# Transposing second attention's first rows one product earlier, and giving each row tile of the last expert block its own PSUM bank

## The chip, the cores and the metric

The kernel runs on one core of a Trainium2 chip. Time is device time in microseconds (us) for one execution; lower is better. TensorE (PE) multiplies, VectorE (DVE) and ScalarE (ACT) work elementwise, GpSimd (POOL) does small arithmetic and issues the indirect DMAs, SyncE (SP) issues the other DMAs. Each engine works through its own instructions in the order in which they are written; semaphores are all that ties the engines together.

## What is computed

Two layers of a gated network over `x` of 4 batches x 1024 tokens x 256. The lines that matter here:

```
x = x + tanh(g_xattn[0]) * L0_xattn(layernorm(x), ctx)      # first attention
x = x + tanh(g_ffn[0])   * L0_ffn(layernorm(x))             # 8 experts, top 2 of each token
x = x + tanh(g_xattn[1]) * L1_xattn(layernorm(x), ctx)      # second attention: 16 heads, 77 keys
x = x + tanh(g_ffn[1])   * L1_ffn(layernorm(x))             # 8 experts, each takes its 256 best tokens

# second attention
sim  = einsum('bhid,bhjd->bhij', x @ Wq, ctx @ Wk) * SCALE
out  = softmax(sim) @ (ctx @ Wv);   return out @ Wo + bo
# second expert layer
out.at[bidx, idx].add(gating * ((silu(x_in @ Wg) * (x_in @ Wu)) @ Wd))
```

## The kernel before, in words

The program has six stages in each engine's stream, one after another: first attention, first experts, a stage named `prep_*` that prepares weights for second attention, second attention (`attn1_*`), the rest of a choice of tokens (`topk_*`), second experts (`ffn1_*`). Nothing but semaphores separates the stages.

All products are made of half-precision pieces. A value v becomes a high piece (ACT copies it to f16) and a low piece (DVE subtracts the high one from v), and `mm3` (L121 to L126) multiplies high by high, high by low and low by high: three matmuls on lines L124, L125, L126. So almost every tile goes PE -> ACT -> DVE before the next product can read it.

**The end of `prep_*`.** For each batch b and half m, PE forms `M1` (folded query and key weights, in four banks `psM`) and then "turns" v of the output weights, `N1` (folded value and output weights), each in one of four banks `psN`. Turns 0 and 1 belong to m = 0, turns 2, 3 and 4 to m = 1. Turn 4, the last one, is the product over the 13 left-over keys of each head and takes 24 matmuls of 256 columns; turns 2 and 3 take 6 each. ACT makes the high piece of each turn (L1336, semaphore `u_nh`), DVE the low piece (`outputs_low`, L1382, semaphore `u_nl`). When b = 3 is complete, `u_nl` stands at 20.

**The beginning of `attn1_*`.** Rows go through in 32 tiles t of 128 tokens. For a tile: DVE takes statistics of the row tile (`stats`, `moments`), POOL makes 1/std (`rstd_of`, L1651 and L1653), DVE normalises (`normalise`, L1859, tile `xn`), PE transposes (L1760, tile `psXar`, whose first half is called `psXa`), ACT and DVE make the pieces `xh` (`high_in`, L1695) and `xl` (`low_in`, L1865), PE forms the scores in two halves (`scores0`, `scores1`, tile `psS`), DVE takes each head's largest score (`largest`, L1880) and ACT the exponentials (`exps`, L1720); then POOL divides (`normalise_probs`, tile `pn`), PE transposes the probabilities (L1798) and multiplies by `N1` (tile `psOL`).

Each engine's order within a step is a table written by hand (`PE_ORDER`, `ACT_ORDER`, `DVE_ORDER`, `POOL_ORDER`) of names with a lag: an entry with lag 2 handles tile t - 2 in step t. In PE's table `scores1` has lag 0 and `scores0` lag 1, so tile 0's half 1 is the first product of the stage, then come the transposes of tile 1, then tile 0's half 0. In DVE's table tile 0's `largest1` stands in step 2, behind `normalise_in` of tile 1 (step 1) and `stats_in` and `moments_in` of tile 2.

Tile 0's statistics and normalisation stand ahead of the tables, woven into the last turns:

```
stats(0)(0, 0)
moments(0)(0, 0)
outputs_low(dve, B - 1, N_TURNS[KD - 1][0])
normalise(0)(0, 0)
for v in N_TURNS[KD - 1][1:]:
    outputs_low(dve, B - 1, v)
```

POOL has, after the 1/std of tile 0 and ahead of the 1/std of tile 1, a wait for all output weights and six small set-up instructions:

```
rstd_of(0)(0, 0)
pool.wait_ge(u_nl, 5 * B)
```

**The end of `ffn1_*`.** The 16 expert blocks have 512 gathered rows each, that is four row tiles n of 128. `down` multiplies the hidden values by the down weights, 24 matmuls of 256 columns for each row tile, into `psYb`, which has four tiles of 128x256 in two PSUM banks: tiles 0 and 1 in one, 2 and 3 in the other. PE and ACT don't touch one bank at the same time, so PE reports (`d_y`) after tiles 1 and 3, and ACT (`results`, L2220) then scales two tiles each into `yo` and reports each (`d_yo`). POOL (`add`, L2118) waits for each row tile's `d_yo` and issues one indirect DMA that adds its rows to `out_x`. Ahead of a block's four adds POOL waits until all adds of the block before have landed (`d_out`). `psXb` is the two-bank tile in which gathered rows are transposed; its last use is for block 15's rows, ahead of that block's up product.

Of the kernel before, what the change touches and what calls it, by code (L numbers as in the profile page):

```python
# [28 lines left out]
ACT = mybir.ActivationFunctionType  # L29
AX = mybir.AxisListType  # L30

P = 128
# [17 lines left out]
SV = 64.0  # L50
# [95 lines left out]
def program(nc, a, out, tab, n0_rows, x1_rows, n_rows):  # L146
    ctx = ExitStack()
    with ctx:
# [1099 lines left out]
        def prep_tensor(pe):  # L1248
# [20 lines left out]
            for b in range(B):  # L1269
                keys = slice(b * LK, (b + 1) * LK)  # L1270
                for m in range(KD):
                    for bank in range(4):
# [7 lines left out]
                        last.then_inc(u_m, 1)  # L1280
                    for v in N_TURNS[m]:
                        if b == 0 and v < 4:
                            pe.wait_ge(u_pl, HP + max(2 * v + 2, v + 5))
                            pe.wait_ge(u_z, 4)
                        wait(pe, u_nl, 5 * b + v - 3)
                        o = psN[(5 * b + v) % 4]
                        for i in range(2):
                            if v < 4:
                                pair = 2 * v + i
                                last = mm3(pe, o[:, i, :], V1[0][:, pair, b, :], V1[1][:, pair, b, :],  # L1290
                                           woh[:, pair * D:(pair + 1) * D], wol[:, pair * D:(pair + 1) * D], True, True)
                                continue
                            first = i * (HP // 2)
                            for pair in range(first, first + HP // 2):
                                last = mm3(pe, o[:, i, :], V2[0][:, pair, b, :], V2[1][:, pair, b, :],
                                           woh[:, pair * D:(pair + 1) * D], wol[:, pair * D:(pair + 1) * D],
                                           pair == first, pair == first + HP // 2 - 1)
                        last.then_inc(u_n, 1)

        def prep_scalar(act):  # L1300
# [20 lines left out]
            for b in range(B):  # L1321
                for m in range(KD):
# [11 lines left out]
                    for v in N_TURNS[m]:  # L1334
                        act.wait_ge(u_n, 5 * b + (v + 1))
                        act.activation(N1[:, b, 2 * v:2 * v + 2, 0:D], psN[(5 * b + v) % 4][:, :, :], ACT.Copy,  # L1336
                                       scale=SV / (SK * SW)).then_inc(u_nh, 1)

# [351 lines left out]
        def attn1_scalar(act):  # L1690
# [52 lines left out]
            steps = dict(weights_high=weights_high, shares_exp=shares_exp, shares_copy=shares_copy,  # L1743
                         high_in=high_in, copy_out=copy_out, exps0=exps(0), exps1=exps(1),
                         probs_high0=probs_high(0), probs_high1=probs_high(1),
                         probs_high2=probs_high(2))
            in_order(act, steps, ACT_ORDER, T, straight=True)

        def attn1_tensor(pe):
# [75 lines left out]
            def digit_odd(t, par):  # L1825
                if odd_of(t) is not None:
# [3 lines left out]
            N1f = N1[:].rearrange("p b c d -> p (b c d)")  # L1830
            steps = dict(tail_a=tail("a"), tail_b=tail("b"), digit_odd=digit_odd, transposes_in=transposes(0), transposes_out=transposes(1), scores0=scores(0), scores1=scores(1),
                         turn0=turn(0), turn1=turn(1), turn2=turn(2), logits=logits,
# [4 lines left out]
        def attn1_vector(dve):  # L1837
# [14 lines left out]
            def normalise(n):  # L1852
                def run(t, par):
# [7 lines left out]
                return run  # L1861

            def low_in(t, par):
# [50 lines left out]
            normalise(0)(0, 0)  # L1914
            for v in N_TURNS[KD - 1][1:]:
                outputs_low(dve, B - 1, v)
            def shares_max(t, par):
# [57 lines left out]
            def weights_low(t, par):  # L1975
                f = t - 4
                if not 0 <= f < FT1:
# [12 lines left out]
                         normalise_in=after_first(normalise(0)), normalise_out=normalise(1), stats_in=after_first(stats(0)), stats_out=stats(1),  # L1990
                         moments_in=after_first(moments(0)), moments_out=moments(1), low_in=low_in,
                         residual=residual, reciprocals=reciprocals)
# [48 lines left out]
                 (7, "n1"): FILL, (7, "n2"): TURN}  # L2041
        ONE_HOT_STEP = 7

        def later(step, name):
# [79 lines left out]
        def ffn1_tensor(pe):  # L2124
# [28 lines left out]
            def down(j, ph):  # L2153
# [3 lines left out]
                for n in range(NT):  # L2157
                    if n % 2 == 0:
                        wait(pe, d_yo, NT * (j - 1) + n + 2 if not isinstance(j, int) or j > 0 else 0)
                    rows = slice(n * P, (n + 1) * P)  # L2160
                    for f in range(FT1):
                        at = f * D
                        last = mm3(pe, psYb[:, n, :], hh1[:, par, f, rows], hl1[:, par, f, rows], W1dh[:, par, at:at + D],
                                   W1dl[:, par, at:at + D], f == 0, f == FT1 - 1)
                    if n % 2 == 1:
                        last.then_inc(d_y, 1)
# [8 lines left out]
        def ffn1_scalar(act):  # L2175
# [36 lines left out]
            def results(j, ph):  # L2212
                par = ph % 2
                if not isinstance(j, int) or j >= 2:
                    act.wait_ge(d_out[par], 16 * NT * (j // 2))
                act.wait_ge(d_gate, j + 1)
                for n in range(NT):
                    if n % 2 == 0:
                        act.wait_ge(d_y, 2 * j + (n // 2 + 1))
                    act.activation(yo1[:, par, n, :], psYb[:, n, :], ACT.Copy, scale=gsc[:, ph, n:n + 1]).then_inc(d_yo, 1)  # L2220

# [177 lines left out]
```

## Time and profile before

| | |
|---|---|
| time, three runs | 1417.0, 1421.34, 1421.36 us, median 1421.34 |
| the profiled execution's own time | 1407.95 us |
| its span in the trace | 1406.2 us, so 1.75 us lie outside the span |
| PE busy | 1297.4 us (92%) |
| DVE, ACT, POOL busy | 911.0, 761.5, 627.0 us |
| mean granted TensorE clock | 0.945 of full speed |

The profile is of one execution. In a timeline a row gives the start and the duration in us, the engine, the line of the kernel, what is written and read, how many instructions the row merges, and in brackets how long the engine had been idle and which engine's instruction ended that wait. A row of windows gives a stretch of the span, its length, the busy time (and number of instructions) of PE, PEld (weight loads), DVE, ACT and POOL in this order, the TensorE clock that was granted (1.00 is 2.4 GHz, 0.50 is 1.2 GHz), the share of DMA busy and GB/s.

### The profile page before, as it was taken

The numbers are of one execution on the slowest core, as the hardware profiler recorded it, in microseconds if no ns is written. First come the engines' busy times: TensorE is split into PE (matmuls) and PEld (weight loads), VectorE is DVE, ScalarE is ACT, GpSimd is POOL, SyncE is SP. The second block draws the span as 40 slices with busy tenths as digits, with TensorE's granted clock in tenths as the row PEclk, the third lists the DMA queues.
The fourth block names the chain that finished last, engine by engine and source line by source line (L and its number), as shares of the span: only waits on it lengthen the run. The fifth ranks groups of instructions, "written<-read, shape, count | busy, mean of one in ns | idle before, by whom it ended". The sixth has DMA issues, their size and how long they took to land.

```text
span 1406.2 us, 29217 instructions
## 1 busy us (share of the span) xinstructions
PE 1297.4 (92%) x9858; PEld 975.7 (69%) x9859; DVE 911.0 (65%) x2128; ACT 761.5 (54%) x2315; POOL 627.0 (45%) x664
## 2 busy tenths in 40 slices
PE   7966699999999999899999985899999999999997
PEld 3755588879999968788888773356656666566555
DVE  2887664565555577778776885777776555566651
ACT  3775332432332365988887752655645555555551
POOL 2177678666666540454444433133333333333113
PEclk8675599999999999999999996999999999999999
DMA  4657444654334351100210103244444444444322
GB/s 146 213 163 184 96 50 56 122 109 67 63 60 64 63 142 40 39 32 32 91 39 24 34 31 93 106 120 121 121 121 124 150 158 148 126 130 129 108 45 31
DMA packets 81546, 133.17 MB, mean 95 GB/s; under 512 B 24662, under 2 KB 71260, under 8 KB 76316
## 3 DMA queue, kind: packets, MB, share of 16 engines
q1 hardware_dynamic: 51132, 93.92, 20.1%
q0 software_dynamic: 29312, 37.57, 16.5%
q8 instruction: 61, 1.00, 0.3%
q14 instruction: 49, 0.40, 0.1%
q10 hardware_dynamic: 992, 0.27, 0.1%
HBM read 95.08 MB, written 36.65 MB: 94 GB/s over the span
## 4 chain that ended last, share of the span: by engine, by line
PE 70%; DVE 10%; DMA 6%; issue 5%; POOL 5%; ACT 2%; SPq 0%; POOLq 0%; ACTq 0%; DVEq 0%
PE psG L124 5%; PE psG L126 5%; PE psG L125 5%; PE psU L124 5%; PE psU L126 5%; PE psU L125 5%; PE psYb L124 4%; PE psYb L125 4%; PE psYb L126 4%; DMA stage<-in_w 3%; PE psP L1798 2%; PE psS L124 2%; PE psS L125 2%; PE psS L126 2%; PE psOL L126 2%
## 5 line engine op out<-in xcount | busy, mean ns | idle before, releaser
L2118 POOL DMA_INDIRECT out_x<-yo,gidx x64 | 100.2, 1566 | 324.0 <-ACT yo L2220 310.8
L2268 DVE SCALAR_TENSOR_TENSOR hid<-psU,sil 128x512 f32<-128x512 f32 x128 | 88.4, 691 | 167.2 <-ACT sil L2209 166.7
L980 POOL DMA_INDIRECT x_rows<-yo,tabs x78 | 124.7, 1599 | 91.7 <-ACT yo L1052 68.0
L1720 ACT ACTIVATE pr<-psS,mx 128x77 f32<-128x77 f32 x512 | 158.8, 359 | 5.2 <-DVE mx L1889 5.2
L2209 ACT ACTIVATE sil<-psG 128x512 f32<-128x512 f32 x128 | 76.4, 597 | 118.1 <-PE psU L126 118.1
L126 PE MATMUL psYb<-W1dh,hl 128*128 128x256 f16 x512 | 139.6, 273 | 0.0
L125 PE MATMUL psYb<-W1dl,hh 128*128 128x256 f16 x512 | 139.6, 273 | 0.0
L124 PE MATMUL psYb<-W1dh,hh 128*128 128x256 f16 x512 | 139.6, 273 | 0.0
L1079 DVE SCALAR_TENSOR_TENSOR hid<-psU,sil 128x512 f32<-128x512 f32 x78 | 53.8, 690 | 127.3 <-ACT sil L1043 127.2
L1720 ACT ACTIVATION_READ_ACCUMULATOR pr<-psS,mx 128x1 f32 x512 | 123.6, 242 | 0.0
L1043 ACT ACTIVATE sil<-psG 128x512 f32<-128x512 f32 x78 | 46.5, 596 | 134.2 <-PE psU L126 132.2
L970 POOL DMA_INDIRECT bx<-n_rows,tabs x78 | 84.6, 1084 | 26.0 <-issue 22.6
L1651 POOL TENSOR_SCALAR rs<-mv 128x1 f32<-128x1 f32 x64 | 14.2, 222 | 180.8 <-DVE mv L1849 180.7
L2103 POOL DMA_INDIRECT gx<-n_rows,gidx x64 | 68.4, 1068 | 47.4 <-DVE gxl L2261 23.6
L124 PE MATMUL psG<-bxh,Wh 128*128 128x256 f16 x312 | 85.7, 275 | 3.9 <-DVE bxl L1070 3.9
L2220 ACT ACTIVATE yo<-psYb,gsc 128x256 f32<-128x256 f32 x64 | 26.8, 470 | 115.1 <-PE psYb L126 115.1
L124 PE MATMUL psOL<-N,pt 128*128 128x256 f16 x320 | 87.3, 273 | 0.7 <-DVE pt L1872 0.7
L125 PE MATMUL psOL<-N,pt 128*128 128x256 f16 x320 | 87.2, 273 | 0.0
L126 PE MATMUL psOL<-N,pt 128*128 128x256 f16 x320 | 87.2, 273 | 0.0
L2281 DVE TENSOR_TENSOR hl<-hid,hh 128x512 f16<-128x512 f32 x128 | 87.2, 681 | 0.0
L125 PE MATMUL psG<-bxl,Wh 128*128 128x256 f16 x312 | 85.7, 275 | 0.0
L126 PE MATMUL psG<-bxh,Wl 128*128 128x256 f16 x312 | 85.7, 275 | 0.0
(407 smaller groups left out, 4331.1 us busy)
## 6 DMA issues: line engine op xcount, KB each, us to landing
w1u<-in_w SPq DMA_DIRECT2D x16, 2048.0 KB, 7.4
w1d<-in_w SPq DMA_DIRECT2D x16, 1024.0 KB, 9.7
stage<-in_w SPq DMA_DIRECT2D x8, 1536.0 KB, 8.9
X<-in_x SPq DMA_DIRECT2D x8, 512.0 KB, 8.6
n_rows<-xc SPq DMA_DIRECT2D x8, 512.0 KB, 9.0
x_rows<-X SPq DMA_DIRECT2D x8, 512.0 KB, 10.2
X<-x_rows SPq DMA_DIRECT2D x8, 512.0 KB, 8.0
out_x<-X SPq DMA_DIRECT2D x32, 128.0 KB, 1.7
```

Of the source, the lines that this page charges most:

```text
L124: pe.matmul(o, lh, rh, start=first, stop=False)
L125: pe.matmul(o, lh, rl, start=False, stop=False)
L126: return pe.matmul(o, ll, rh, start=False, stop=stop)
L970: pool.indirect_dma_start(bx[:, par, n, :], None, n0_rows[:, :], bass.IndirectOffsetOnAxis(tabs[:, j, n, 0:1], 0)).then_inc(b_in[par], 16)
L980: pool.indirect_dma_start(x1_rows[:, :], bass.IndirectOffsetOnAxis(tabs[:, j, n, 0:1], 0), yo[:, par, n, :], None, compute_op=ALU.add).the ...
L1079: dve.scalar_tensor_tensor(hid[:, half, :, :], psU[half][:, :, :], SH / (SX * SW), sil[:, half, :, :], ALU.mult, ALU.mult).then_inc(b_hid[ ...
L1720: ins = act.activation(pr1[:, par, h * LK:(h + 1) * LK], psS1[:, q, i * LK:(i + 1) * LK], ACT.Exp, bias=mx1[:, h:h + 1], scale=1.0 / (SX * ...
L2103: pool.indirect_dma_start(gx[:, j % 2, n, :], None, n_rows[0:2 * S * (j // E + 1), :], bass.IndirectOffsetOnAxis(gidx[:, half, col:col + 1 ...
L2118: pool.indirect_dma_start(out_rows[:, :], bass.IndirectOffsetOnAxis(gidx[:, half, col:col + 1], 0), yo1[:, j % 2, n, :], None, compute_op= ...
L2209: act.activation(sil1[:, f % 2, :], psG1[f % 2][:], ACT.Silu, scale=1.0 / (SX * SW)).then_inc(d_sil, 1)
L2268: dve.scalar_tensor_tensor(hid1[:, f % 2, :], psU1[f % 2][:], SH / (SX * SW), sil1[:, f % 2, :], ALU.mult, ALU.mult).then_inc(d_hid, 1)
L2281: dve.tensor_tensor(hl1[:, par, f, :], hid1[:, f % 2, :], hh1[:, par, f, :], ALU.subtract).then_inc(d_hl, 1)
```

## The change

Part one, at the seam between `prep_*` and `attn1_*`: PE's two transposes of tile 0 are issued ahead of turn 4 of batch 3, not behind it, and wait for `c_xn[0]` (tile 0 normalised) and for `u_nl` at 17 (bank free). ACT's `high_in` of tile 0 stands ahead of the high piece of turn 4, and DVE's `low_in` of tile 0 between the low pieces of turns 3 and 4. The tables skip tile 0 for these three. Part two, in the last expert block only: row tiles 0 to 3 go into four banks (`psYb` twice, `psXb` twice), PE reports after each of them, and ACT waits for each.

```
--- before.py
+++ after.py
@@ prep_tensor
                     for v in N_TURNS[m]:
+                        if b == B - 1 and v == 4:
+                            pe.wait_ge(c_xn[0], 1)
+                            pe.wait_ge(u_nl, 5 * b + 2)
+                            for k in range(KD):
+                                last = pe.transpose(psXa[:, k, :], xn1[0][:, 0, k * P:(k + 1) * P], ident[:])
+                            last.then_inc(c_xt[0], 1)
                         if b == 0 and v < 4:
@@ prep_scalar
                     for v in N_TURNS[m]:
-                        act.wait_ge(u_n, 5 * b + (v + 1))
-                        act.activation(N1[:, b, 2 * v:2 * v + 2, 0:D], psN[(5 * b + v) % 4][:, :, :], ACT.Copy,
-                                       scale=SV / (SK * SW)).then_inc(u_nh, 1)
+                        if b < B - 1 or v < 4:
+                            outputs_high(act, b, v)
@@ attn1_scalar
+            high_in(0, 0)
+            outputs_high(act, B - 1, 4)
             in_order(act, steps, ACT_ORDER, T, straight=True)
@@ attn1_vector
-            for v in N_TURNS[KD - 1][1:]:
-                outputs_low(dve, B - 1, v)
+            outputs_low(dve, B - 1, 3)
+            low_first()
+            outputs_low(dve, B - 1, 4)
@@ ffn1
+        def result(j, n):
+
+            if j == NB1 - 1:
+                return (psYb[:, 0, :], psYb[:, 2, :], psXb[:, 0, 0:D], psXb[:, 1, 0:D])[n]
+            return psYb[:, n, :]
@@ ffn1_tensor, down
                 for n in range(NT):
-                    if n % 2 == 0:
+                    if j == NB1 - 1:
+                        pe.wait_ge(d_yo, NT * (j - 1) + 2 * min(n, 1) + 2)
+                    elif n % 2 == 0:
                         wait(pe, d_yo, NT * (j - 1) + n + 2 if not isinstance(j, int) or j > 0 else 0)
...
-                    if n % 2 == 1:
+                    if n % 2 == 1 or j == NB1 - 1:
                         last.then_inc(d_y, 1)
@@ ffn1_scalar, results
                 for n in range(NT):
-                    if n % 2 == 0:
+                    if j == NB1 - 1:
+                        act.wait_ge(d_y, 2 * j + n + 1)
+                    elif n % 2 == 0:
                         act.wait_ge(d_y, 2 * j + (n // 2 + 1))
```

In PE's stream, at the end of `prep_*` (psN2 and psN3 are the banks of turns 3 and 4, psXar that of the transposes, xn10 tile 0 normalised), the change puts the two transposes (x2) between the products of turns 3 and 4:

```order
 L125 MATMUL psN2<-wo1l,V1h 128x256
 L126 MATMUL psN2<-wo1h,V1l 128x256
+L1286 MATMUL psXar<-ident,xn10 128x128 x2
 L124 MATMUL psN3<-wo1h,V2h 128x256
 L125 MATMUL psN3<-wo1l,V2h 128x256
```

They stood on line L1760 behind the 24 matmuls of turn 4, directly ahead of the first scores.

DVE's stream from tile 0's statistics to tile 0's first `largest`, before the change (psN1, psN2 and psN3 are the banks of turns 2, 3 and 4; `st10`, `mv10`, `rs10`, `xn10` belong to the normalisation in front of the scores):

```order
L1843 BN_STATS st10<-X 128x6
L1849 BN_AGGR mv10<-st10 128x2
L1382 SCALAR_TENSOR_TENSOR N1<-psN1,N1 128x2x256
L1859 TENSOR_SCALAR xn10<-X,mv10,rs10 128x256
L1382 SCALAR_TENSOR_TENSOR N1<-psN2,N1 128x2x256
L1382 SCALAR_TENSOR_TENSOR N1<-psN3,N1 128x2x256
L1843 BN_STATS st10<-X 128x6
L1849 BN_AGGR mv10<-st10 128x2
L1865 SCALAR_TENSOR_TENSOR xl1<-psXar,xh1 128x256
L1859 TENSOR_SCALAR xn10<-X,mv10,rs10 128x256
L1843 BN_STATS st10<-X 128x6
L1849 BN_AGGR mv10<-st10 128x2
```

And the same stretch of the changed kernel, up to that `largest`:

```order
L1393 SCALAR_TENSOR_TENSOR N1<-psN2,N1 128x2x256
L1881 SCALAR_TENSOR_TENSOR xl1<-psXar,xh1 128x256
L1393 SCALAR_TENSOR_TENSOR N1<-psN3,N1 128x2x256
L1856 BN_STATS st10<-X 128x6
L1862 BN_AGGR mv10<-st10 128x2
L1872 TENSOR_SCALAR xn10<-X,mv10,rs10 128x256
L1856 BN_STATS st10<-X 128x6
L1862 BN_AGGR mv10<-st10 128x2
L1896 TENSOR_REDUCE psS1<-psS1 128x2x4
L1905 TENSOR_SCALAR mx1<-psS1 128x8
```

The low piece of tile 0 (`xl1`) has moved ahead of turn 4's low piece; all else keeps its order. POOL's stream is the same in both.

## Rows read from the trace of the kernel before

**Rows 1.** The page: the span, and each engine's busy time.

```profile
span 1406.2 us, 29217 instructions
PE 1297.4 (92%) x9858; PEld 975.7 (69%) x9859; DVE 911.0 (65%) x2128; ACT 761.5 (54%) x2315; POOL 627.0 (45%) x664
```

**Rows 2.** Windows, all of second attention.

```profile
555.00:850.00 295.00, 273.93 (x2322) 230.75 (x2319) 231.38 (x614) 228.06 (x1198) 132.48 (x233) 0.99 0.13 43
```

**Rows 3.** Timeline of PE at the seam.

```profile
552.46 0.27 PE L124 MATMUL psN<-wo1h,V2h 128*128 128x256 f16 x1
...
554.97 0.27 PE L126 MATMUL psN<-wo1h,V2l 128*128 128x256 f16 x1
556.04 0.41 PE L1760 MATMUL psXar<-ident,xn 128*128 128x128 f32 x2 [0.79 <-DVE xn L1859]
558.00 0.44 PE L124 MATMUL psS<-M1h,xh 128*128 128x308 f16 x1 [1.55 <-DVE xl L1865]
...
561.06 0.45 PE L1760 MATMUL psXar<-ident,xn 128*128 128x128 f32 x2
561.35 0.29 PE L124 MATMUL psS<-M1h,xh 128*128 128x308 f16 x1
...
565.05 0.29 PE L124 MATMUL psS<-M1h,xh 128*128 128x308 f16 x1 [1.97 <-ACT pr L1720]
```

**Rows 4.** Timeline of POOL at the seam.

```profile
557.15 0.20 POOL L1678 MEMSET ones<- 128x128 bf16 x1 [1.71 <-DVE N L1382]
...
558.92 0.58 POOL L1653 TENSOR_TENSOR rs<-rs,mhalf 128x1 f32<-128x1 f32 x1
```

**Rows 5.** Timeline of DVE at the seam.

```profile
555.48 0.42 DVE L1859 TENSOR_SCALAR xn<-X,mv,rs 128x256 f32<-128x256 f32 x1 [0.45 <-POOL rs L1653]
555.80 1.28 DVE L1382 SCALAR_TENSOR_TENSOR N<-psN,N 128x512 f16<-128x512 f32 x2
...
559.53 0.41 DVE L1859 TENSOR_SCALAR xn<-X,mv,rs 128x256 f32<-128x256 f32 x1 [1.59 <-POOL rs L1653]
...
560.32 0.18 DVE L1849 BATCH_NORM_AGGREGATE mv<-st 128x2 f32<-128x6 f32 x1
561.30 0.81 DVE L1880 TENSOR_REDUCE psS<-psS 128x8 f32<-128x616 f32 x1 [0.80 <-PE psS L126]
```

**Rows 6.** Timeline of ACT at the seam: turn 4's high piece.

```profile
555.28 0.60 ACT L1336 ACTIVATE N<-psN 128x512 f16<-128x512 f32 x1 [1.70 <-PE psN L126]
```

**Rows 7.** The chain that ended last, one piece (start, us, what).

```profile
562.35 2.57 ACT pr L1720 x16
```

**Rows 8.** Windows of 1 us at the seam, columns as in rows 2.

```profile
557.00:558.00 1.00, 0.00 (x0) 0.00 (x0) 0.91 (x4) 0.00 (x0) 0.64 (x4) 0.89 0.00 0
558.00:559.00 1.00, 1.00 (x4) 0.59 (x5) 0.00 (x0) 0.00 (x0) 0.69 (x5) 0.50 0.01 4
...
561.00:562.00 1.00, 1.00 (x9) 0.80 (x8) 0.70 (x1) 0.38 (x1) 0.46 (x1) 0.91 0.92 393
```

**Rows 9.** Windows around PE's longest wait, at second attention's end, columns as in rows 2.

```profile
845.00:850.00 5.00, 0.00 (x0) 0.00 (x0) 4.86 (x5) 0.00 (x0) 0.00 (x0) 0.79 0.00 0
850.00:855.00 5.00, 3.98 (x26) 3.85 (x26) 2.17 (x6) 0.38 (x1) 0.79 (x2) 0.50 0.15 52
```

**Rows 10.** Timeline of ACT at the very end: the last two row tiles.

```profile
1395.82 0.84 ACT L2220 ACTIVATE yo<-psYb,gsc 128x256 f32<-128x256 f32 x2 [4.32 <-PE psYb L126]
```

**Rows 11.** Timeline of POOL at the very end: the adds.

```profile
1387.93 1.54 POOL L2118 DMA_INDIRECT out_x<-yo,gidx  x1 [0.30 <-issue]
1392.93 1.54 POOL L2118 DMA_INDIRECT out_x<-yo,gidx  x1 [3.46 <-DMA out_x<-yo,gidx]
...
1396.62 1.54 POOL L2118 DMA_INDIRECT out_x<-yo,gidx  x1 [0.30 <-ACT yo L2220]
1398.46 1.54 POOL L2118 DMA_INDIRECT out_x<-yo,gidx  x1 [0.30 <-issue]
```

**Rows 12.** The DMAs that write out_x: from issue to landing.

```profile
DMA to landing us min/median/max: 1.7/3.8/8.3
```

More of the change, by code:

```diff
@@ L1334, in prep_scalar, with outputs_high @@
                     for v in N_TURNS[m]:
-                        act.wait_ge(u_n, 5 * b + (v + 1))
-                        act.activation(N1[:, b, 2 * v:2 * v + 2, 0:D], psN[(5 * b + v) % 4][:, :, :], ACT.Copy,
-                                       scale=SV / (SK * SW)).then_inc(u_nh, 1)
+                        if b < B - 1 or v < 4:
+                            outputs_high(act, b, v)
+        def outputs_high(act, b, v):
+            act.wait_ge(u_n, 5 * b + (v + 1))
+            act.activation(N1[:, b, 2 * v:2 * v + 2, 0:D], psN[(5 * b + v) % 4][:, :, :], ACT.Copy,
+                           scale=SV / (SK * SW)).then_inc(u_nh, 1)
         def prep_vector(dve):
@@ L1743, in attn1_scalar @@
             steps = dict(weights_high=weights_high, shares_exp=shares_exp, shares_copy=shares_copy,
-                         high_in=high_in, copy_out=copy_out, exps0=exps(0), exps1=exps(1),
+                         high_in=after_first(high_in), copy_out=copy_out, exps0=exps(0), exps1=exps(1),
                          probs_high0=probs_high(0), probs_high1=probs_high(1),
                          probs_high2=probs_high(2))
+            high_in(0, 0)
+            outputs_high(act, B - 1, 4)
             in_order(act, steps, ACT_ORDER, T, straight=True)
@@ L1830, in attn1_tensor @@
             N1f = N1[:].rearrange("p b c d -> p (b c d)")
-            steps = dict(tail_a=tail("a"), tail_b=tail("b"), digit_odd=digit_odd, transposes_in=transposes(0), transposes_out=transposes(1), scores0=scores(0), scores1=scores(1),
+            steps = dict(tail_a=tail("a"), tail_b=tail("b"), digit_odd=digit_odd, transposes_in=after_first(transposes(0)), transposes_out=transposes(1), scores0=scores(0), scores1=scores(1),
                          turn0=turn(0), turn1=turn(1), turn2=turn(2), logits=logits,
@@ L1861, in normalise, with low_first @@
                 return run
+            def low_first():
+                low_in(0, 0)
             def low_in(t, par):
@@ L1990, in attn1_vector @@
                          normalise_in=after_first(normalise(0)), normalise_out=normalise(1), stats_in=after_first(stats(0)), stats_out=stats(1),
-                         moments_in=after_first(moments(0)), moments_out=moments(1), low_in=low_in,
+                         moments_in=after_first(moments(0)), moments_out=moments(1), low_in=after_first(low_in),
                          residual=residual, reciprocals=reciprocals)
@@ L2162, in down @@
                         at = f * D
-                        last = mm3(pe, psYb[:, n, :], hh1[:, par, f, rows], hl1[:, par, f, rows], W1dh[:, par, at:at + D],
+                        last = mm3(pe, result(j, n), hh1[:, par, f, rows], hl1[:, par, f, rows], W1dh[:, par, at:at + D],
                                    W1dl[:, par, at:at + D], f == 0, f == FT1 - 1)
-                    if n % 2 == 1:
+                    if n % 2 == 1 or j == NB1 - 1:
                         last.then_inc(d_y, 1)
@@ L2217, in results @@
                 for n in range(NT):
-                    if n % 2 == 0:
+                    if j == NB1 - 1:
+                        act.wait_ge(d_y, 2 * j + n + 1)
+                    elif n % 2 == 0:
                         act.wait_ge(d_y, 2 * j + (n // 2 + 1))
-                    act.activation(yo1[:, par, n, :], psYb[:, n, :], ACT.Copy, scale=gsc[:, ph, n:n + 1]).then_inc(d_yo, 1)
+                    act.activation(yo1[:, par, n, :], result(j, n), ACT.Copy, scale=gsc[:, ph, n:n + 1]).then_inc(d_yo, 1)
             def hidden_high(f):
```

## The prediction

> **What bounds the kernel now.** I read the page first. TensorE is busy 1297.4 of 1406.2 us [rows 1], so whatever holds PE up at a place where nothing else is queued for it lengthens the kernel. A second look, at the windows, says how far that holds in second attention: 273.9 of 295 us busy [rows 2]. So a delay at the mouth of that stage is carried to its end, since PE has little slack in which to win it back. Both parts of the change lie where the average doesn't reach: at a seam between two stages and in the last microseconds. So the views to use are the timelines of each engine there, together with the releaser in brackets.
>
> At the seam, PE's timeline [rows 3] shows turn 4 of the output weights from 552.46 to 555.24 (last start 554.97 plus 0.27), a wait of 0.79 for `xn` of tile 0, the transposes at 556.04, a wait of 1.55 for `xl`, and then the first twelve score matmuls from 558.00 to 561.06. Those twelve take 0.255 us each; the next twelve start at 561.35 and end at 563.08 (565.05 less the wait of 1.97), 0.131 each. The windows of the same stretch explain it: the granted clock falls to half at about 557.8 (0.89 of the window 557 to 558), is 0.50 at 558 to 559 and comes back at about 561.2 [rows 8]. This is what the change seems made for: two waits and a half-clock stretch around the first scores.
>
> But what set the time of everything behind? The first `largest` of DVE starts at 561.30 and has waited 0.80 for PE [rows 5]; from there the chain runs through sixteen instructions of exponentials at 562.35 [rows 7] and on to POOL's division. So the stage's clock is the start of that `largest`, and it has two inputs. One is PE's scores. The other is DVE's own queue: ahead of it stand `xn` of tile 1 (559.53, having waited 1.59 for POOL's 1/std) and the statistics of tile 2, done at 560.32 + 0.18 = 560.50 [rows 5]. This second input is only 0.80 us behind the first.
>
> Where does the 1/std of tile 1 come from? POOL first waits for all output weights (`u_nl` at 20), released by the low piece of turn 4, which ends at 555.80 + 1.28 = 557.08; its set-up starts at 557.15 and tile 1's 1/std is done at 558.92 + 0.58 = 559.50 [rows 4, 5]. So there is a path turn 4 -> high piece -> low piece -> six set-up instructions and 1/std on POOL -> `xn` of tile 1 -> statistics of tile 2 -> `largest` of tile 0. The change delays the head of this path.
>
> **Part one, step by step.** *The transposes.* They are put ahead of turn 4 but need `xn` of tile 0, which ends at 555.48 + 0.42 = 555.90 [rows 5]. Nothing ahead of that on DVE or POOL is touched. So they start at 556.04 as before. PE, which had begun turn 4 at 552.46, now stands idle from there to 556.04: 3.6 us of work that used to lie in the shadow of this wait (2.8 of it turn 4) is pushed behind it. Matmuls keep their written order, so turn 4 can't slip past.
>
> *Turn 4.* It starts behind the transposes, 0.29 later as at 561.06 to 561.35 [rows 3]: 556.33. Its length is bounded from both sides. At full clock it takes its 2.78 and ends at 559.1. At half clock throughout, its starts spread by the ratio of the score matmuls, 0.255 / 0.131 = 1.95: 2.51 x 1.95 + 0.3 = 5.2, end at 561.5. Which? A wait of 1.97 left the clock full (565.05); waits of 0.79 and 1.55 with 0.41 of work between brought it to half, and so did the longest wait, from before 845 to after 850 [rows 3, 8, 9]. The new wait, 3.3 us unbroken (552.7 to 556.04), is nearer to the two that cost the clock. If it falls where it fell before, at 557.8, 13 of the 24 run at 0.109 and the rest at 0.213, and turn 4 ends at 560.2; I take a little more, 560.3.
>
> *Its pieces.* ACT starts the high piece 0.04 after PE ends and takes 0.60 [rows 6]; DVE's low piece follows in about 0.03 and 0.68 (two took 1.28 [rows 5]). That is 1.35, so `u_nl` stands at 20 at 560.45, 561.6 or 562.9 for the three ends, against 557.08.
>
> *POOL and what is queued behind.* The step to POOL's first set-up instruction is 0.07; from there to DVE being free for `largest` it was 560.50 - 557.15 = 3.35 [rows 4, 5], and none of that changes. So `largest` starts at 563.9, 565.0 or 566.3, against 561.30: **+2.6, +3.7 or +5.0 us**. The 0.80 that `largest` used to wait for PE is already in these differences.
>
> *PE's side.* The first scores now follow turn 4 without a wait (their `xl` is made at about 557.3, under turn 4), and even at half clock end 3.2 us after it, at 564.7 against a `largest` at 566.3. So PE is no longer what ends that wait. This is the gain that the change is to bring: with a full clock the scores end at 560.7, not 561.2. It buys nothing, because DVE isn't there yet. PE then waits for `xn` of tile 1 before the second transposes, at about 563.3 at the earliest, and only then makes tile 0's other scores. These take 1.7 us at full clock, ending at 565.4, at half clock at 566.9. The first exponentials run until 1.05 + 2.57 after the first `largest` starts [rows 5, 7], until 567.5; the second half needs 1.05 from its scores to its exponentials, so it is ready at 566.5 or 568.0. This adds 0 to 0.5; I take 0.
>
> *Covered pieces.* `high_in` ahead of turn 4's high piece on ACT and `low_in` ahead of its low piece on DVE (0.4 us each) cost nothing: both run while PE is in turn 4. If turn 4 were done by then, they would cost 0.8. SP also waits for `u_nl`: the bias row and the first load of second expert weights leave some 4 us later; the first is needed by tile 0's last outputs and the second some steps on, and neither ends a wait now.
>
> **Part two.** The last block's tiles would be copied one at a time, so tiles 0 and 2 earlier by one tile's product (24 x 0.109 = 2.6 us), tile 1 no earlier, and tile 3 from 1395.82 + 0.84 to + 0.48 [rows 10]. But POOL's four last adds start at 1392.93, released by the landing of block 14's last add (issued 1387.93), and follow at 1.84 apiece to 1398.46 [rows 11]. Tile 2's add at 1396.62 came when POOL was free (1394.77 + 1.54 + 0.30), and its tile was ready at 1395.82 + 0.42 + 0.3 = 1396.5. So the early tiles would wait for POOL; the gain is 0 to 0.1. POOL's pace is bounded by a landing: here 4.73 (1387.93 to 0.27 before 1392.93), elsewhere 1.7 to 8.3, median 3.8 [rows 12]. With 3.8 the four would start at 1392.0, tile 2's add no longer would wait for PE, and the change would gain 0.9. If the landing is short enough, tile 3 itself decides: add at 1395.82 + 0.48 + 0.3 = 1396.6, not 1398.46, a gain of at most 1.8.
>
> The Trainium skill, DMA: Bandwidth & Descriptors, section Anatomy of one DMA, gives a DMA issued from GpSimd about 2.0 us fixed and bytes over 436 GB/s; for 128 rows of 1 KB that is 2.3 us, and by it the full 1.8 us would be gained here. This case's trace disagrees: 4.73 us for this very add.
>
> **The sum.** Part one +3.7, part two 0: the profiled execution would go from a span of 1406.2 to 1409.9, and with the 1.75 outside it from 1407.95 to 1411.65. That execution is 13 us faster than the median of the timed runs, 1421.34; the seam is a chain of compute durations, so I carry the difference over as it is: 1425.0 us.
>
> **Rivals.**
> *A, half clock almost throughout (slower, +4.3 to +5.5).* The new wait costs the clock before turn 4 begins, and perhaps again in the wait before the second transposes. For it: the length of the wait. Against: the half-clock stretch before lasted 3.4 us, so turn 4 may get its end at full clock. It decides once turn 4 ends after 560.8. 1425.6 to 1426.8.
> *B, the cover pays (not slower).* Scores end at 560.7, the wait for `xl` is gone, and the stage starts 0.5 to 0.7 earlier: 1420.7. The point from which it decides is POOL: its wait for `u_nl` at 20 would have to end by 557.4 (560.8 less 3.35 and 0.07), and for any gain at all by 557.9. Turn 4 is still under way then. I leave it a chance only for what the trace may hide, such as a wait that isn't where I read it.
> *C, the tail gives back 0.9 to 1.8.* A landing nearer the median than the 4.73 of this add: +3.7 less the middle of the two, 1423.6; with a full clock and the whole 1.8, +0.8, 1422.1. The figure of the Trainium skill (above) would put the time at this end.
> *D, neither part shows.* Should DVE or POOL win the delay back inside second attention: 1421.3. Against it: 93% busy PE.
>
> **How the numbers follow.** About 0.3%, 4.3 us, is what a measurement of this kernel can tell from no change (its three runs span 4.4). Forecast (+2.6 to +4.3) 0.50; A 0.28; C 0.10; B 0.05; D 0.07. The range 1420.0 to 1428.5 holds A and C whole and the scatter of a median above A; below it lies what is left of B and D with scatter. Slower by over 0.3%: most of A and a part of the forecast's upper half, 0.37. Within: 0.57. Faster by over 0.3%: only scatter on B, C or D, 0.06.
>
> **What the profile after would show.** Right: PE idle about 3.3 us ahead of the transposes, released by `xn`; turn 4 behind them; no wait of the first scores for `xl`; POOL's first set-up at 560.5 to 563; DVE's first `largest` behind the statistics of tile 2, not behind PE, at 564 to 566; PE waiting for `xn` of tile 1; POOL's four last adds still 1.84 apart, their first released by a landing. Wrong: `xn` of tile 0 well before 555.9 after the stage's start, which would make the move free; a first `largest` within 1 us of where it was; or a tail whose adds wait for tiles.

## The result, and the profile after

| | median | runs |
|---|---|---|
| before | 1418.33 us | 1416.21 to 1421.48, 20 runs |
| changed kernel | 1423.88 us | 1420.04 to 1426.46, 20 runs |

The ratio is 1.0038, with a 95% interval of 1.003 to 1.0045: **the change costs 5.5 us (4.3 to 6.4)**. The forecast was +3.7 on a median of 1421.34, which is 1425.0; the measured 1423.88 lies in the range of 1420.0 to 1428.5. One timed execution of all kernels below stood apart, 2899.41 us in e9, and is in no ratio.

The profiled execution of the changed kernel has a span of 1420.3 us, 14 more than the one before. Most of this says nothing about the change: tile 0's normalisation, which comes ahead of everything that was moved, starts at 565.32 in the one and at 555.48 in the other [rows 5], and over all the profiles below it lies anywhere from 553.5 to 571.8. So every seam here is measured from that instruction; its start is called x0. The rest of the comparison is made with differences from x0.

The timeline of PE at the seam of the changed kernel (start, duration, line, tile, in brackets the idle time and its releaser):

```profile
562.19 0.27 PE L126 MATMUL psN<-wo1h,V1l 128*128 128x256 f16 x1
565.79 0.56 PE L1286 MATMUL psXar<-ident,xn 128*128 128x128 f32 x2 [3.32 <-DVE xn L1872]
566.14 0.42 PE L124 MATMUL psN<-wo1h,V2h 128*128 128x256 f16 x1
...
569.34 0.30 PE L124 MATMUL psN<-wo1h,V2h 128*128 128x256 f16 x1
...
570.24 0.27 PE L126 MATMUL psN<-wo1h,V2l 128*128 128x256 f16 x1
570.35 0.29 PE L124 MATMUL psS<-M1h,xh 128*128 128x308 f16 x1
...
574.78 0.44 PE L1773 MATMUL psXar<-ident,xn 128*128 128x128 f32 x2 [2.70 <-DVE xn L1872]
...
578.91 0.29 PE L124 MATMUL psS<-M1h,xh 128*128 128x308 f16 x1 [2.12 <-ACT pr L1731]
```

It answers to rows 3. The two short waits (0.79 and 1.55) are gone, and the scores at 570.35 start without one. In their place stand one wait of 3.32 ahead of the transposes, a turn 4 whose matmuls start 0.21 apart for the first 15 and 0.11 apart after that, and a wait of 2.70 for tile 1's normalisation. The windows of 1 us show the clock (the column ahead of the last two) at half under turn 4, and once more at 580:

```profile
565.00:566.00 1.00, 0.21 (x2) 0.22 (x3) 0.68 (x2) 0.00 (x0) 0.28 (x1) 0.98 0.00 0
566.00:567.00 1.00, 1.00 (x7) 0.69 (x6) 0.53 (x2) 0.38 (x1) 0.00 (x0) 0.50 0.06 16
...
569.00:570.00 1.00, 1.00 (x9) 0.82 (x8) 0.00 (x0) 0.00 (x0) 0.00 (x0) 0.81 0.00 0
570.00:571.00 1.00, 1.00 (x10) 0.79 (x9) 0.00 (x0) 0.45 (x1) 0.00 (x0) 1.00 0.00 0
...
580.00:581.00 1.00, 1.00 (x5) 0.61 (x4) 0.00 (x0) 1.00 (x8) 0.00 (x0) 0.50 0.00 0
```

Now what the rest waited for. The timeline of POOL, then that of DVE:

```profile
571.93 0.20 POOL L1689 MEMSET ones<- 128x128 bf16 x1 [6.65 <-DVE N L1393]
...
573.70 0.58 POOL L1664 TENSOR_TENSOR rs<-rs,mhalf 128x1 f32<-128x1 f32 x1
```

```profile
565.32 0.41 DVE L1872 TENSOR_SCALAR xn<-X,mv,rs 128x256 f32<-128x256 f32 x1 [0.45 <-POOL rs L1664]
...
571.18 0.69 DVE L1393 SCALAR_TENSOR_TENSOR N<-psN,N 128x512 f16<-128x512 f32 x1 [3.95 <-ACT N L1347]
...
574.31 0.41 DVE L1872 TENSOR_SCALAR xn<-X,mv,rs 128x256 f32<-128x256 f32 x1 [1.90 <-POOL rs L1664]
...
575.10 0.18 DVE L1862 BATCH_NORM_AGGREGATE mv<-st 128x2 f32<-128x6 f32 x1
575.20 0.78 DVE L1896 TENSOR_REDUCE psS<-psS 128x8 f32<-128x616 f32 x1
```

Read it as one path: low piece of turn 4 at 571.18, POOL's first set-up at 571.93 (it had waited 6.65 for it), tile 1's 1/std done at 574.28, `xn` of tile 1 at 574.31, the first `largest` at 575.20. That `largest` has no bracket: nothing but its own queue held it, while PE's scores had long been there (the last of them starts at 571.79). In before it waited 0.80 for PE [rows 5]. From x0 it is 9.88 us, against 5.82.

The second-attention stage then carries the delay to its end. The line of the residuals (one for each of the 32 row tiles, first and last start), before:

```profile
L1905 DVE SCALAR_TENSOR_TENSOR X<-psOL,thx,X x32: 447/478/486, 579.0 to 850.2; 128x256 f32<-128x256 f32 x32
```

and in the changed kernel:

```profile
L1921 DVE SCALAR_TENSOR_TENSOR X<-psOL,thx,X x32: 450/478/486, 593.7 to 864.9; 128x256 f32<-128x256 f32 x32
```

Less x0 the last is at 294.7 before and 299.6 after: +4.9 us, of which 4.06 are the first `largest` and 0.8 come behind it. The rest of the program passes this on: from there to the end of the span it is 556.0 us before (1406.2 less 850.2) and 555.4 after (1420.3 less 864.9).

At the very end, POOL's adds of the changed kernel:

```profile
1402.70 1.54 POOL L2141 DMA_INDIRECT out_x<-yo,gidx  x1 [0.30 <-issue]
1407.21 1.54 POOL L2141 DMA_INDIRECT out_x<-yo,gidx  x1 [2.96 <-DMA out_x<-yo,gidx]
...
1412.74 1.54 POOL L2141 DMA_INDIRECT out_x<-yo,gidx  x1 [0.30 <-issue]
```

ACT's last four copies, now one at a time, start at 1402.81, 1405.35, 1407.97 and 1410.59. The adds don't follow them: the first is released by the landing of block 14's last add, as in [rows 11], and the last starts 2.15 after the last tile's copy starts, against 2.27 before (1398.46 less 1396.19; the row of 1395.82 in [rows 10] merges two copies).

### The profile page after: what moved, and what is told of

It is laid out like the page before. It is cut to its first block, busy times and chain, and to the rows that moved or that the text cites. A ratio compares the mean times of both kernels' runs of the same rounds, so it can differ in the third digit from the quotient of the medians.

```text
span 1420.3 us, 29218 instructions
## 1 busy us (share of the span) xinstructions
PE 1300.5 (92%) x9858; PEld 976.1 (69%) x9859; DVE 911.7 (64%) x2128; ACT 760.7 (54%) x2315; POOL 625.2 (44%) x664
## 4 chain that ended last, share of the span: by engine, by line
PE 72%; DVE 11%; DMA 5%; issue 4%; POOL 4%; ACT 3%; another core or an unknown queue 1%; SPq 0%; DVEq 0%; ACTq 0%; POOLq 0%
PE psG L124 6%; PE psG L126 5%; PE psG L125 5%; PE psU L125 5%; PE psU L124 5%; PE psU L126 5%; PE psYb L124 4%; PE psYb L126 4%; PE psYb L125 4%; PE psP L1811 2%; PE psS L124 2%; PE psS L126 2%; PE psS L125 2%; DMA stage<-in_w 2%; PE psOL L126 2%
## 5 line engine op out<-in xcount | busy, mean ns | idle before, releaser
L126 PE MATMUL psYb<-W1dh,hl 128*128 128x256 f16 x496 | 135.2, 273 | 0.0
L125 PE MATMUL psYb<-W1dl,hh 128*128 128x256 f16 x496 | 135.2, 273 | 0.0
L124 PE MATMUL psYb<-W1dh,hh 128*128 128x256 f16 x496 | 135.2, 273 | 0.0
L124 PE MATMUL psY<-Wh,hh 128*128 x312 | 85.1, 273 | 1.0 <-issue 0.9
L126 PE MATMUL psU<-bxh,Wl 128*128 128x256 f16 x312 | 85.6, 274 | 0.1
L125 PE MATMUL psU<-bxl,Wh 128*128 128x256 f16 x312 | 85.6, 274 | 0.1
```

Source lines behind the costliest of these rows:

```text
L124: pe.matmul(o, lh, rh, start=first, stop=False)
L125: pe.matmul(o, lh, rl, start=False, stop=False)
L126: return pe.matmul(o, ll, rh, start=False, stop=stop)
```

## The experiments

All but one were timed against before on the same chip, in rounds. The table gathers what each trace shows, from x0 where not said otherwise; "clock" is what the granted clock was under the first long product behind the new or the old wait. "Last residual" is the end of the seam's reach, "last add" the start of the program's last add after the start of the last tile's copy. A ratio rests on 12 executions of the kernel, in e2 on 5, in e3 on 11, in e10 on 7. The groups of runs had different chips, so ratios compare across groups and times don't.

| run | ratio to before (95%) | clock | first `largest` | last residual | last add |
|---|---|---|---|---|---|
| before | | half | 5.82 | 294.7 | 2.27 |
| before, second trace (e11) | | half | 5.81 | 294.7 | 2.63 |
| changed kernel | 1.0038 (1.003 to 1.0045) | half, 3.4 us | 9.88 | 299.6 | 2.15 |
| e1 part two alone | 0.9995 (0.9985 to 1.0004) | half | 5.82 | 294.7 | 2.10 |
| e2 part one alone | 1.0038 (1.0025 to 1.0051) | half throughout | 10.91 | 299.8 | 2.22 |
| e3 + tile 1 early | 1.0014 (1.0002 to 1.0027) | half throughout | 8.10 | 297.9 | |
| e4 + wait filled | 1.0037 (1.0024 to 1.0051) | full | 8.22 | 297.9 | |
| e5 both of these | 1.0000 (0.9983 to 1.0017) | full | 5.35 | 295.0 | |
| e10 as e3, POOL as changed | 1.0043 (1.002 to 1.0066) | full | 8.22 | 297.9 | |
| e6 before, DVE and POOL order | 0.9987 (0.9972 to 1.0002) | full | 3.71 | 292.6 | |
| e7 before, banks for two blocks | 0.9980 (0.9964 to 0.9997) | full | 4.95 | 293.8 | 0.75 |
| e8 e6, e7 and filled waits | 0.9986 (0.997 to 1.0003) | full | 3.71 | 292.6 | 1.03 |
| e9 e6 and e7 | 0.9987 (0.9969 to 1.0004) | half | 5.08 | 294.0 | 0.75 |
| e12 e8 again | 0.9975 (0.9959 to 0.999) | full | 3.71 | 293.6 | 1.04 |

**e1, part two alone.** Before with the second half of the diff.

> Part two alone: before, with only the last block's four row tiles in four banks. Theory S (the loss is all at the seam): no measurable change, 0 to 0.9 us faster; the four last adds start by a landing and follow 1.84 apart. Rival T (some of the 5.5 us come from the tail, for instance copies that meet the matmuls of another bank): slower by 1 to 5 us, with a gap between the last adds.

Measured: no change can be seen (1405.49 against 1406.03 us). The adds start 1.84 apart behind a landing, the last at 1398.20, though ACT had the tiles one by one. There is nothing of the loss at this end, nor a gain that can be told from zero (the interval leaves 2.1 us faster to 0.6 slower): Theory S holds, Rival T is out.

**e2, part one alone.** The changed kernel with the old end.

> Part one alone: the changed kernel with the old tail. Theory S: as slow as the whole change, 4.5 to 5.5 us above before; first largest 9.9 us after the start of tile 0's normalisation, against 5.8 before. Rival T: 0 to 3 us above before.

Measured: 1412.02 against 1406.03 us, the whole of the loss. Here the clock was low from ahead of turn 4 to its end and the first `largest` came at 10.91, a microsecond later than expected. With a landing 0.7 shorter than in before (4.01, not 4.73), two tiles to a bank do show: the third add waits for its tile.

```profile
1396.39 1.54 POOL L2141 DMA_INDIRECT out_x<-yo,gidx  x1 [2.73 <-DMA out_x<-yo,gidx]
1398.23 1.54 POOL L2141 DMA_INDIRECT out_x<-yo,gidx  x1 [0.30 <-issue]
1400.75 1.54 POOL L2141 DMA_INDIRECT out_x<-yo,gidx  x1 [0.97 <-ACT yo L2247]
```

That 0.67 (0.97 less 0.30) is an estimate of what part two can be worth in such an execution; the times don't show it.

**e3, tile 1 early.** Does the delay travel through POOL and tile 1? The changed kernel, with (tables skip tile 1 too):

```
@@ POOL
             rstd_of(0)(0, 0)
+            rstd_of(0)(1, 1)
             pool.wait_ge(u_nl, 5 * B)
@@ DVE
             outputs_low(dve, B - 1, 3)
+            stats(0)(1, 1)
+            moments(0)(1, 1)
             low_first()
+            normalise(0)(1, 1)
             outputs_low(dve, B - 1, 4)
```

> The changed kernel, but tile 1's statistics, 1/std and normalisation stand ahead of turn 4's low piece on DVE and ahead of the wait for all output weights on POOL. Theory S (the delayed turn 4 reaches DVE's first largest through POOL and tile 1): first largest then follows PE's scores, 6.9 us after the start of tile 0's normalisation (9.9 in the changed kernel, 5.8 in before); time 1 to 2 us above before, 3 to 4 below the changed kernel. Rival C (the half clock of turn 4 and of the scores is what costs, POOL's path is only seen beside it): largest stays at 9 to 10 us and the time within 1 us of the changed kernel.

Measured: 1408.09 against 1406.03 us, +0.14% where the changed kernel has +0.38%, so some 60% of the loss is gone by the ratios. (The trace is of the slowest of the 11 executions, and in it the last residual is 1.7 earlier than in the changed kernel's, a third of the 4.9.) Tile 1 is normalised at 2.58 and no longer in the way. The number for `largest` was missed, 8.10 instead of 6.9, because the clock was at half throughout and turn 4 ended a microsecond later than in the changed kernel. DVE's rows also show something that Theory S had left out:

```profile
563.40 0.69 DVE L1401 SCALAR_TENSOR_TENSOR N<-psN,N 128x512 f16<-128x512 f32 x1 [3.95 <-ACT N L1355]
564.01 0.42 DVE L1865 BATCH_NORM_STATS2 st<-X 128x6 f32<-128x256 f32 x1
564.46 0.18 DVE L1871 BATCH_NORM_AGGREGATE mv<-st 128x2 f32<-128x6 f32 x1
564.56 0.78 DVE L1905 TENSOR_REDUCE psS<-psS 128x8 f32<-128x616 f32 x1
```

`largest` has no bracket. With tile 1 out of the way it stands directly behind turn 4's low piece and the statistics of tile 2, about 0.2 behind PE's scores (564.08 + 0.29 = 564.37). So the low piece is an obstacle by itself, a small one.

**e4, the wait filled.** The changed kernel, with work for PE while it waits for `xn`:

```
@@ PE, ahead of the transposes
                         if b == B - 1 and v == 4:
+                            pe.wait_ge(u_nl, 5 * b + v - 3)
+                            for f in range(28):
+                                pe.matmul(psN[(5 * b + v) % 4][:, f % 2, :], V2[0][:, f % HP, b, :],
+                                          woh[:, (f % HP) * D:(f % HP + 1) * D], start=True, stop=True)
                             pe.wait_ge(c_xn[0], 1)
```

> The changed kernel with 28 matmuls of 256 columns more, whose results are overwritten, in PE's wait ahead of the transposes, so that the wait is filled with work. Theory S: turn 4 runs at full clock (2.8 us, not 4.7), all else of the path stays, so the first largest comes 8.4 us after the start of tile 0's normalisation (9.9 without them) and the time is 1.5 to 2.5 us below the changed kernel, still 2.6 to 3.5 above before. Rival C: with the clock kept, all of the loss is gone, 0 to 1 us above before. A third case: the clock is lost all the same, time as the changed kernel.

Measured: in the trace it does what Theory S says. The wait shrinks to 0.26, turn 4 runs at full clock, `largest` comes at 8.22 (expected 8.4), and the last residual is at 297.9, 3.3 later than before:

```profile
553.99 0.44 PE L1290 MATMUL psXar<-ident,xn 128*128 128x128 f32 x2 [0.26 <-DVE xn L1876]
554.27 0.27 PE L124 MATMUL psN<-wo1h,V2h 128*128 128x256 f16 x1
554.38 0.27 PE L125 MATMUL psN<-wo1l,V2h 128*128 128x256 f16 x1
```

So the clock alone doesn't explain the loss (Rival C is out). But the timed runs, 1412.10 against 1406.03, don't show the 1.5 to 2.5 us below the changed kernel. The two intervals, 1.0024 to 1.0051 here and 1.003 to 1.0045 there, leave room for no more than 3 us; the trace's difference in last residual, 1.7 us (0.12%), is within them, the same time for both is nearer their middle. e2, with the same seam and timed beside e4 on one chip, has 1412.02. The gain from filling is seen in the trace and not in the times. Why the times don't show it stays open: the clock of the executions without a trace isn't known stretch by stretch.

**e5, both.** The changed kernel with e3's and e4's edits.

> The changed kernel with both mendings: tile 1's statistics and normalisation ahead of turn 4's low piece, and the 28 overwritten matmuls in PE's wait. Theory S: turn 4 starts 0.6 after the start of tile 0's normalisation and ends at 3.6, the scores at 5.0, and the first largest starts at 5.1 to 5.3 (before 5.8, changed kernel 9.9 to 10.9); the stage's last residual 0.7 us earlier to 0.3 later than before, or up to 1 us later if PE's clock falls once more behind it; time within 1 us of before. Rival C: POOL's path doesn't matter beside the clock; then this is as the kernel with the filled wait alone, 3.3 us later than before in the trace.

Measured: 1420.87 against 1420.45 us, ratio 1.0000 (0.9983 to 1.0017): with both mended the loss is gone. `largest` comes at 5.35 behind the low piece and two statistics, not behind the scores; the last residual at 295.0, 0.4 later than before although `largest` was 0.5 earlier, since PE's clock fell once more further on (0.50 at 11 to 12 after x0). Rival C would have had 3.3. What the filling adds to e3's edit isn't clear of zero in the times: the intervals of e3 and e5 overlap.

**e10, POOL's order put back.** Is it POOL's wait, or DVE's statistics behind the low piece? e3 with this:

```
@@ POOL
             rstd_of(0)(0, 0)
-            rstd_of(0)(1, 1)
             pool.wait_ge(u_nl, 5 * B)
...
             ch.end()
+            rstd_of(0)(1, 1)
@@ DVE
-            normalise(0)(1, 1)
             outputs_low(dve, B - 1, 4)
+            normalise(0)(1, 1)
```

> The run e3 with one thing put back: POOL makes tile 1's 1/std behind its wait for all output weights, as in before and in the changed kernel (DVE's normalisation of tile 1 therefore behind turn 4's low piece; its statistics stay early). Theory S: the link is POOL's wait, so all of what e3 won is lost: first largest 3.3 us after POOL's first set-up instruction, at 9.9 to 10.9 after the start of tile 0's normalisation, and the time 4 to 6 us above before. Rival D (the link is DVE's statistics of tile 1 behind the low piece, not POOL): largest at 7 to 8.1 as in e3, time 1 to 3 above before.

Measured: 1415.20 against 1409.57 us, ratio 1.0043 (e3 1.0014; the intervals just overlap, from 1.002 to 1.0027), all of what e3 won is lost. In its trace the statistics of tile 1 are done at 556.33 + 0.18, five microseconds ahead of their use, and still:

```profile
561.67 0.58 POOL L1672 TENSOR_TENSOR rs<-rs,mhalf 128x1 f32<-128x1 f32 x1
```

```profile
562.28 0.41 DVE L1881 TENSOR_SCALAR xn<-X,mv,rs 128x256 f32<-128x256 f32 x1 [2.45 <-POOL rs L1672]
562.61 0.42 DVE L1865 BATCH_NORM_STATS2 st<-X 128x6 f32<-128x256 f32 x1
563.07 0.18 DVE L1871 BATCH_NORM_AGGREGATE mv<-st 128x2 f32<-128x6 f32 x1
563.17 0.77 DVE L1905 TENSOR_REDUCE psS<-psS 128x8 f32<-128x616 f32 x1
```

The link is POOL's wait and set-up: `xn` of tile 1 was released by POOL after an idle 2.45, and `largest` starts 3.3 after POOL's first set-up (8.22 less 4.94), as expected. The absolute number was missed again (8.22 and not 9.9 or more; by itself it lies next to Rival D's 7 to 8.1), since this execution kept its clock and POOL's set-up began at 4.94, though the wait ahead of the transposes was the same 3.32. That gives clean pairs at equal clock: 8.22 against e5's 5.35 at full clock, 10.91 (e2) against 8.10 (e3) at half. **POOL's path costs 2.9 and 2.8 us.** And pairs at equal order: 10.91 against 8.22, 8.10 against 5.35: half clock under turn 4 and the scores costs 2.7 us when it lasts throughout.

**e6, the idea the other way round.** If DVE's queue was the hidden second bound of before, reordering it alone should gain. Before, PE and ACT untouched, with:

```
@@ DVE
-            for v in N_TURNS[KD - 1][1:]:
-                outputs_low(dve, B - 1, v)
+            outputs_low(dve, B - 1, 3)
+            stats(0)(1, 1)
+            moments(0)(1, 1)
+            low_in(0, 0)
+            outputs_low(dve, B - 1, 4)
+            normalise(0)(1, 1)
```

and `rstd_of(0)(1, 1)` on POOL as in e3.

> Before, with DVE's and POOL's order alone changed: tile 0's low piece ahead of turn 4's low piece, tile 1's statistics and 1/std ahead of both waits; PE and ACT as before. Theory S (what the first scores waited for in before was DVE's queue): scores start 2.0 us after the start of tile 0's normalisation, not 2.5; first largest 5.2 to 5.5, not 5.8; time 0.3 to 0.6 us below before. Rival: the earlier start only meets more of the half clock, or the low piece of turn 4, now later, holds POOL; no gain or a loss of up to 0.5.

Measured: 1418.66 against 1420.45 us, ratio 0.9987 with an interval that just takes in 1. The scores start at 1.93, as expected, and `largest` at 3.71, earlier than the 5.2 to 5.5 expected, because the clock stayed full here; it is now released by PE:

```profile
572.33 0.81 DVE L1889 TENSOR_REDUCE psS<-psS 128x8 f32<-128x616 f32 x1 [0.17 <-PE psS L134]
```

That is 1.2 ahead of before's seam at full clock (e7's trace, 4.95, where `largest` has no idle ahead of it, so that DVE's queue alone held it):

```profile
573.87 0.77 DVE L1880 TENSOR_REDUCE psS<-psS 128x8 f32<-128x616 f32 x1
```

In e9, whose clock fell at the same place, it is 5.08 against 5.82, 0.7 ahead.

**e7, banks for two blocks.** If a landing holds the last adds, the block to speed up is 14, not 15. Before, with part two for both (the lines shown are against part two as in the changed kernel):

```
+        FOUR = NB1 - 2
...
-            if j == NB1 - 1:
+            if j >= FOUR:
                 return (psYb[:, 0, :], psYb[:, 2, :], psXb[:, 0, 0:D], psXb[:, 1, 0:D])[n]
...
+                    if j > FOUR:
+                        pe.wait_ge(d_yo, NT * (j - 1) + n + 1)
```

> Before, with four banks for the last two expert blocks, 14 and 15, not for the last alone. Theory L (the landing of block 14's last add sets the end): block 14's adds go out as its tiles come, the last 1.8 us earlier, so block 15's adds start 1.8 us earlier and the kernel ends 1.5 to 1.9 us earlier. Rival P: the four last adds are held by their own tiles or by POOL; 0 to 0.3.

Measured: 1418.63 against 1420.45 us, ratio 0.9980, an interval below 1. Block 14's last add goes out at 1398.76, its landing releases the four of block 15, and the last two wait for their tiles:

```profile
1398.76 1.54 POOL L2126 DMA_INDIRECT out_x<-yo,gidx  x1 [1.08 <-ACT yo L2234]
1402.71 1.54 POOL L2126 DMA_INDIRECT out_x<-yo,gidx  x1 [2.40 <-DMA out_x<-yo,gidx]
1404.55 1.54 POOL L2126 DMA_INDIRECT out_x<-yo,gidx  x1 [0.30 <-issue]
1406.62 1.54 POOL L2126 DMA_INDIRECT out_x<-yo,gidx  x1 [0.53 <-ACT yo L2234]
1409.24 1.54 POOL L2126 DMA_INDIRECT out_x<-yo,gidx  x1 [1.08 <-ACT yo L2234]
```

The last add starts 0.75 after the last tile's copy starts, not 2.27: 1.5 us. In before that copy is the second of two in a row; from the end of PE's last matmul the last add starts 0.78 here (1409.24 less 1408.46) and 2.68 in before (1398.46 less 1395.78), so the end of the program gains 1.9. By the medians the kernel gains 1.8 us, by the ratio 2.8. Theory L holds. This trace's seam is that of before with the clock kept, which before's own two traces don't show.

**e8 and e12, all of it, with PE's waits filled; e9, without the filling.** e8 is e6 and e7 with 7 and 9 matmuls into a free bank around the transposes.

> Before with DVE's and POOL's order of the run e6, four banks for the last two blocks, and 7 and 9 overwritten matmuls in PE's two waits around the transposes of tile 0 (behind turn 4, as in before). Theory S: the first scores run at full clock, from 2.0 to 3.6 us after the start of tile 0's normalisation; first largest at 3.7 to 3.9, 2.0 us ahead of before; with the end's 1.8 the time is 3 to 4 us below before. Rival C-: a later wait costs the clock that these kept, and the gain at the seam is 0 to 1, the whole 2 to 3.

> The DVE and POOL order of the run e6 and four banks for the last two blocks, without the overwritten matmuls. Theory S and L together: first largest 1.2 us ahead of a before whose clock stays and 2.1 ahead of one whose clock falls; the last add of the program starts 1.3 to 1.5 us sooner after PE's last product; time 2 to 3.5 us below before. Rival: the two gains are given back by later landings or by the stages between; within 1 us of before.

> The run e8 once more, beside e9 on one chip: with a clock that was kept at this seam in two traces anyway, the overwritten matmuls should make no difference to e9 (within 1 us). If the clock falls at this seam in a good part of the timed runs, e12 is 0.5 to 1 us below e9.

Measured: e8 0.9986, e9 0.9987, e12 0.9975 (1405.71 against 1409.57 us, interval 0.9959 to 0.999). So this version is faster than the changed kernel, and than before by some 2 to 4 us; only e12's interval lies below 1, those of e8 and e9 take it in. The expected 3 to 4 us were reached in e12 (3.5 by the ratio) and not in e8 (2.0), the same kernel. The seam with the filling did what was expected (3.71 in both traces). Without it the clock fell in e9's trace and `largest` came at 5.08, 0.7 ahead of before and not 2.1. Two things took some back. In e12 the clock fell 8 us after x0, and the last residual stands at 293.6 and not at 292.6. And the landing of block 14's last add took 4.96 in e8 and e12, 3.7 and 3.8 in e7 and e9, so that e8's last add starts 1.03 after its tile's copy. (In e8 and e12 the row of block 15's first add names a copy of ACT as its releaser. That copy is of tile 1, and the tile that this add waits for had been copied 2.5 us earlier, so I take the landing as what released it, as in the other twelve traces.) Whether the filling gains anything isn't settled: e12 and e9 were timed together and their intervals overlap.

**e11, before once more.**

> Before once more, for a second sample of its seam and tail. If the clock falls behind the transposes as in the first trace: first largest 5.8 us after the start of tile 0's normalisation and the last residual 294.7; if it stays, 4.95 and 293.8. The last add starts 2.2 us after the last tile's copy when the landing takes 4.7 us, less with a shorter one.

Measured: the first case, 5.81 and 294.7; the last add 2.63 after the last tile's copy, with a landing of 5.09.

## Why the prediction was right, and where it was off

*What holds the transposes.* Right: `xn` of tile 0 releases them, 0.47 after x0, after an idle 3.32 (predicted 3.3).

*Turn 4.* It was given an end at 560.3, 4.8 after x0, as if the clock fell where it had fallen before. It came 5.19 after x0 in the changed kernel's trace, 6.2 in e2's. The clock fell at the moment at which the work began, not 1.5 us later, so 15 of 24 matmuls ran at 0.21. Mechanism right, size 0.4 to 1.4 short.

*Pieces, POOL, tile 1, `largest`.* Right to 0.1: 1.36 from turn 4's end to `u_nl` at 20 (571.87 less 570.51; predicted 1.35), 0.06 to POOL, then 3.27 to `largest` (575.20 less 571.93; predicted 3.35). The path was shown to be POOL's wait by e3 and e10.

*The second scores.* "This adds 0 to 0.5; I take 0." This term was mis-sized: from the first `largest` to the last residual it is 289.7 to 289.9 in the changed kernel, e3, e4, e5, e10 and e12, and 288.8 to 288.9 in the other eight traces. The 0.8 to 0.9 come with another fall of the clock, absent in those eight: it begins 14.3 us after x0 in the changed kernel and 8.0 to 13.1 in the other five. In the changed kernel it lies under the scores of tile 1, whose wait of 2.12 for the exponentials is followed, five matmuls later, by matmuls 0.26 apart. It wasn't the second scores of tile 0, as the text had it, but the first of tile 1.

*Part two.* Right: 0 to 0.1 by the row, and e1 measures none. Its limit, the landing, was right too (e7). The Trainium skill, DMA: Bandwidth & Descriptors, section Anatomy of one DMA, by whose figure the landing was estimated at 2.3 us, isn't borne out here. The fourteen traces have 3.7 to 5.1 for this add.

*The sum.* +3.7 was forecast; the trace has +4.9 and the times +5.5 (4.3 to 6.4). The trace's 1.2 more are turn 4's end (0.4) and the fall of the clock under tile 1 (0.8). That the forecast time, 1425.0, lies only 1.1 from the measured one is in part luck: the difference was 1.8 short, while the base, a median of three runs, was 3.0 above the median of twenty. By size this is the case called A (+4.3 to +5.5), to which 0.28 was given, and not the forecast's (+2.6 to +4.3). Within 0.3% had the larger chance; slower by over 0.3% is what came. The difference between the trace's 4.9 and the timed 5.5 is inside the interval and needs no cause.

*Rivals B, C and D.* B needed turn 4's pieces by 557.4, 1.9 after x0; they came at 6.55. C wanted 0.9 to 1.8 back from the end of the program; in the changed kernel the last add starts 2.19 after the end of PE's last matmul, against 2.68 before, and these 0.5 are the shorter landing (4.24, that is 1402.70 to 0.27 before 1407.21, against 4.73). For D, the stage gave nothing back.

## What to carry to other kernels

Before moving a small step ahead of a large one, look whether what the small one waits for is there by then. Here it wasn't: the large one's whole length moved behind the wait, and its consumers on an engine that looks idle (POOL, whose wait for "all weights" stood ahead of the next tile's 1/std) became the path. Before moving work on the engine with the visible waits, look at the second-latest input of the instruction that waits: here it was 0.80 us behind, and reordering that queue alone brought the first `largest` forward by 1.2 us at full clock (e6) and by 0.7 at half (e9), though by the times e6's gain isn't clear of zero. At the end of a program, find which transfer releases the last ones and speed up its block, not the last block.

## What was not expected of the hardware

The clock is not a property of the kernel's order alone. The same wait of 3.32 us ahead of the transposes was followed by half clock in the changed kernel, e2 and e3, and by full clock in e10; before's seam has half clock in three traces (before, e1, e11) and full clock in e7. The stretch at half clock isn't of one length either: 3.4 us in the changed kernel, over 6 in e2 and e3, with PE at work from 0.5 after x0 on. At this seam that is worth 0.9 us in before (5.82 against 4.95) and up to 2.7 in the changed order, which makes the changed order not only slower but more exposed.
